# Half-height stacks: each head with 64 rows of its own in both stacks of a fused attention kernel

## The reference

```
scores = q @ k.T / sqrt(8)        # per head, 256 x 256 (short phases: 128 x 128)
attn = softmax(scores)
out = (attn @ v) @ Wo + bo + x    # then a norm
```

## Time and profile before

| | us |
|---|---|
| runs of the kernel (3) | 393.17, 393.67 (median), 396.62 |
| span of the profiled execution | 394.8 |
| TensorE matmul busy | 324.5 |
| VectorE busy | 291.2 |
| ScalarE busy | 233.6 |
| GpSimd busy | 182.8 |
| first maxima step | 35.15 |

### The profile page before, as it was taken

How to read it: one execution, slowest core, us unless ns; L and a number is a source line. 1 busy time by engine, 2 the same in 40 slices (tenths; PEclk the granted TensorE clock), 3 DMA queues, 4 the chain that set the end, 5 groups by cost and what they waited for, 6 DMA issues and landing times.

```text
span 394.8 us, 8256 instructions
## 1 busy us (share of the span) xinstructions
PE 324.5 (82%) x2838; PEld 195.7 (50%) x2838; DVE 291.2 (74%) x622; ACT 233.6 (59%) x502; POOL 182.8 (46%) x259
## 2 busy tenths in 40 slices
PE   0453678999998878969788898799999998999994
PEld 0230144555555546647556776474545544455551
DVE  4783967797995886967796538866888989898711
ACT  0220022767787753837378497468767775786692
POOL 8605015074341657857736255702667657550000
PEclk9995565999999998957899899899999999999998
DMA  7879309051746839189549143603447262544001
GB/s 246 316 94 123 24 9 114 2 95 32 120 67 60 105 47 93 27 109 114 97 61 113 16 84 83 79 2 83 88 51 107 47 77 63 62 87 53 15 3 28
DMA packets 39978, 30.54 MB, mean 77 GB/s; under 512 B 4352, under 2 KB 39040, under 8 KB 39808
## 3 DMA queue, kind: packets, MB, share of 16 engines
q1 hardware_dynamic: 39216, 28.66, 47.8%
q10 hardware_dynamic: 720, 1.35, 1.0%
HBM read 5.55 MB, written 0.52 MB: 15 GB/s over the span
## 4 chain that ended last, share of the span: by engine, by line
PE 47%; DVE 23%; DMA 10%; issue 9%; SPq 5%; ACT 4%; POOL 2%; ACTq 0%; POOLq 0%; DVEq 0%
PE ps_small L854 14%; PE ps_max L854 11%; DVE neg_max L1212 10%; PE ps_score L854 9%; PE ps_heads L854 9%; DMA q_stack<-q_parts 6%; SPq L724 3%; DVE k_parts L644 2%; DMA q_stack<-max_rows 2%; SPq L727 2%; DVE k_parts L642 2%; DVE onehot L1159 2%; PE ps_small L1001 2%; ACT probs L1052 1%; DMA pos_i<-in_pos 1%
## 5 line engine op out<-in xcount | busy, mean ns | idle before, releaser
L1212 DVE TENSOR_REDUCE neg_max<-ps_max 128x2 f32<-128x512 f32 (+1 forms) x256 | 165.1, 686 | 40.6 <-PE ps_max L854 38.3
L1052 ACT ACTIVATE probs<-ps_score 128x512 f32<-128x512 f32 x256 | 136.3, 605 | 43.1 <-PE ps_score L854 42.5
L854 PE MATMUL ps_max<-k_stack,q_stack 96*128 96x512 bf16 (+1 forms) x320 | 99.5, 368 | 22.4 <-DVE neg_max L1212 11.2
L854 PE MATMUL ps_score<-q_stack,k_stack 100*128 100x256 bf16 (+1 forms) x640 | 84.5, 259 | 3.6 <-DMA q_stack<-max_rows 2.6
L854 PE MATMUL ps_heads<-probs,v_cols 128*32 128x256 f32 (+1 forms) x1280 | 70.5, 344 | 0.7 <-ACT probs L1052 0.7
L854 PEld LDWEIGHTS ps_score<-q_stack,k_stack 100*128 100x128 bf16 x640 | 52.7, 101 | 30.4 <-ACT probs L1052 9.7
L641 POOL TENSOR_TENSOR split_r<-q_f,k_parts 64x256 f32<-64x256 f32 x26 | 18.7, 720 | 100.3 <-issue 87.5
L854 PEld LDWEIGHTS ps_max<-k_stack,q_stack 96*128 96x128 bf16 x320 | 28.7, 102 | 64.1 <-DVE neg_max L1212 42.1
L854 PEld LDWEIGHTS ps_heads<-probs,v_cols 128*32 128x32 f32 x1280 | 33.1, 110 | 24.1 <-issue 10.5
L854 PE MATMUL ps_small<-src_t,w 128*128 128x256 f32 x96 | 30.3, 437 | 2.1 <-ACT src_t L1118 1.1
L826 POOL TENSOR_TENSOR rstd<-var_eps,minus_half 128x2 f32<-128x2 f32 x20 | 14.2, 712 | 38.3 <-DVE var_eps L1170 38.1
(11 more groups left out here) (119 smaller groups left out, 446.9 us busy)
## 6 DMA issues: line engine op xcount, KB each, us to landing
k_stack<-k_parts SPq DMA_DIRECT2D x120, 128.0 KB, 4.1
q_stack<-q_parts SPq DMA_DIRECT2D x120, 64.0 KB, 3.8
w<-in_w SPq DMA_DIRECT2D x1, 1024.0 KB, 9.5
rows<-in_rows ACTq DMA_DIRECT2D x1, 704.0 KB, 9.1
w<-in_w SPq DMA_DIRECT2D x1, 576.0 KB, 11.3
pos_i<-in_pos ACTq DMA_DIRECT2D x2, 256.0 KB, 6.2
ctx_t<-in_ctx_t SPq DMA_DIRECT2D x2, 256.0 KB, 8.0
src_t<-in_x_t SPq DMA_DIRECT2D x2, 256.0 KB, 9.1
```

What stands on the lines that cost most here:

```text
L854: return nc.tensor.matmul(out, lhs_t, rhs, start=start, stop=stop, **k)
L1052: nc.scalar.activation(probs[:, n % PROB_BUFS, :], ps_score[n % SCORE_BUFS][:, :], ACT.Exp, scale=SCALE).then_inc(exped, 1)
L1212: nc.vector.tensor_reduce(dst, src, AX.X, ALU.max, negate=True).then_inc(max_taken, 1)
```

## The change

Both stacks get 128 used rows: the 64 rows 64*parity + 8*d + slot belong to one head of the pair, with six slots of parts and two spare ones. Each head so has rows of its own, and a matmul reads one half of the partitions: rows 0 to 63 or 64 to 127, with the array as a tile of 64 rows by 128 columns at row 0 or 64.

- `k_parts` loses its second plane and its zeros, `k_stack` is half as wide: [128, 3, 8 pairs, 256]. A stack DMA writes rows slot, slot+8, ... (16 of them, 4 KB each) for q and for k.
- A max bank is one parity: in long phases one head with both query tiles (two matmuls of 256 columns), in short ones two heads of one parity with both tiles (four of 128). Bank i has parity i mod 2. A score bank is as big as before, in short phases two heads of one parity; bank c has parity c mod 2. The contraction is over 62 rows for the maxima and 64 for the scores.
- The maxima go into rows 62, 63, 126 and 127, by two DMAs. The ones and zeros of the spare rows of both stacks are loaded by four DMAs from an input, ahead of three of the four weight loads; the memsets are gone, and the first max step waits for the loads.
- k's first part is one ACT instruction, its split one step. VectorE does it for unit 0 and phases 1 and 2 (before: unit 0, and half of it in phases 1, 2 and 4).
- The planner's costs: 120 in place of 216 and 218 for max and score steps, 1300 in place of 650 for placing maxima, 720 in place of 1080 for k's ACT work, 1150 in place of 1100 for a split on VectorE, other start times. `WEIGHTS` is the same.

```diff
-SLOT_ROWS = 2 * DH
-MAX_ROW = SLOT_ROWS * len(SLOTS)
-MAX_ROWS = 4
+ROW_SLOTS = 8
+SPARE_SLOTS = (6, 7)
+HALF = P // 2
+MAX_ROW = HALF - 2
...
-SPLIT_ON_DVE = (("k", 1, 0), ("k", 2, 0), ("k", 4, 1))
+SPLIT_ON_DVE = (("k", 1), ("k", 2))
...
-        pe = {"max": 216, "score": 218, "value": 590 if short else 1020, "q": 440, "k": 440, "v": 430,
+        pe = {"max": 120, "score": 120, "value": 590 if short else 1020, "q": 440, "k": 440, "v": 430,
...
-    plan.free.update(dve=11500, pool=14500)
+    plan.free.update(dve=9500, pool=1000)
...
-        k_parts = sb("k_parts", [P, 2, PARTS, 2, T], BF16)
+        k_parts = sb("k_parts", [P, 2, PARTS, T], BF16)
         q_stack = sb("q_stack", [P, STACK_BUFS, PAIRS, T], BF16)
-        k_stack = sb("k_stack", [P, STACK_BUFS, H, T], BF16)
+        k_stack = sb("k_stack", [P, STACK_BUFS, PAIRS, T], BF16)
...
+        def half_rows(par, n=HALF):
+
+            return slice(HALF * par, HALF * par + n)
...
+            for kind, stack in ((0, q_stack), (1, k_stack)):
+                for slot in SPARE_SLOTS:
+                    sp.dma_start(stack[slot::ROW_SLOTS, :, :, :].rearrange("r b h t -> r b (h t)"),
+                                 a["spare"][kind, slot - SPARE_SLOTS[0]].bitcast(BF16).unsqueeze(1).broadcast_to(
+                                     [P // ROW_SLOTS, STACK_BUFS, PAIRS * T])).then_inc(spare_loaded, 16)
...
+                        if (part > 0) == rest:
+                            sp.dma_start(stack_of(kind, u)[slot::ROW_SLOTS, :, :], parts_of(kind, u)[part]
+                                         ).then_inc((q_placed if kind == "q" else k_placed)[buf], 16)
...
+                    for par in range(2):
+                        sp.dma_start(q_stack[HALF * par + MAX_ROW:HALF * (par + 1), u % STACK_BUFS, :, :],
+                                     max_rows[2 * PAIRS * par:2 * PAIRS * (par + 1), u % 2, :]
+                                     ).then_inc(max_placed[u % STACK_BUFS], 16)
...
+                    first_pair, par = divmod(i, 2)
+                    at = half_rows(par, MAX_ROW)
...
-                        last = mm(out[:, :], q_stack[0:MAX_ROW, buf, pair, qt * P:(qt + 1) * P],
-                                  k_stack[0:MAX_ROW, buf, 2 * pair:2 * pair + 2, :].rearrange("p a b -> p (a b)"))
+                        for qt in range(NT):
+                            last = mm(out[:, qt * T:(qt + 1) * T], stack_of("q", u)[at, first_pair, qt * P:(qt + 1) * P],
+                                      stack_of("k", u)[at, first_pair, :])
...
+                    first_pair, par = divmod(c, 2)
+                    at = half_rows(par)
...
                         for kt in range(NT):
-                            last = mm(out[:, kt * T:(kt + 1) * T], k_stack[0:SCORE_ROWS, buf, c, kt * P:(kt + 1) * P],
-                                      q_stack[0:SCORE_ROWS, buf, c // 2, :])
+                            last = mm(out[:, kt * T:(kt + 1) * T],
+                                      stack_of("k", u)[at, first_pair, kt * P:(kt + 1) * P],
+                                      stack_of("q", u)[at, first_pair, :])
...
-                            for half, part in part_views(kind, u):
-                                last = nc.scalar.activation(part[0], ps_small[half, 0:T], ACT.Identity,
-                                                            bias=V(f"b{kind}{phase}")[half, :])
-                            last.then_inc(small_used[n % SMALL_BUFS], 1)
+                            nc.scalar.activation(parts_of(kind, u)[0], ps_small[:, 0:T], ACT.Identity,
+                                                 bias=V(f"b{kind}{phase}")).then_inc(small_used[n % SMALL_BUFS], 1)
```

More of the change, by code:

```diff
@@ L158, in waits @@
                 return [("part", kind[-1], u)]
-            return [("split" + kind[5:], u, half) for half in range(2 if kind == "stack_k" else 1)]
+            return [("split" + kind[5:], u)]
         if st[0] == "small" and self.count["small"] >= SMALL_BUFS:
@@ L294, in append @@
         if kind == "stack_max":
-            done["placed", "max", u] = run("dma", t, 650) + 2000
+            done["placed", "max", u] = run("dma", t, 1300) + 2000
             return
@@ L333, in append @@
             else:
-                t = part = run("act", t, 720 if kind == "q" else 1080)
+                t = part = run("act", t, 720)
             done["part", kind, u] = part
@@ L556, in build @@
         q_split = [sem(f"q_split{i}") for i in range(2)]
-        k_split = [[sem(f"k_split{half}{i}") for i in range(2)] for half in range(2)]
+        k_split = [sem(f"k_split{i}") for i in range(2)]
         base_ready = sem("base_ready")
@@ L622, in first_part_done, with split_done, split @@
             return used(no("small", kind, u)) if u // B else (first_part, 2 * u + turn(kind, u))
[L624 to L632, removed]
+        def split_done(kind, u):
+            return (q_split if kind == "q" else k_split)[u % 2], u // 2 + 1
+        def split(engine, ops, link, kind, u):
             which = 0 if kind == "q" else 1
@@ L638, in split @@
                 engine.wait_ge(s_, 16 * len(SLOTS) * n_)
-            lines, part = part_views(kind, u)[half]
-            full, rest = q_f[lines, u % 2, which, :], split_r[lines, u % 2, which, :]
+            part = parts_of(kind, u)
+            full, rest = q_f[:, u % 2, which, :], split_r[:, u % 2, which, :]
             link(ops.tensor_tensor(rest, full, part[0], ALU.subtract))
             link(ops.tensor_tensor(part[1], full, part[0], ALU.subtract))
-            done = split_done(kind, u, half)
+            done = split_done(kind, u)
             ops.tensor_tensor(part[2], rest, part[1], ALU.subtract).then_inc(done[0], 1)
@@ L1379, in constants @@
 def constants():
+    spare = np.zeros((2, len(SPARE_SLOTS), 2, DH, PAIRS * T), np.float32)
+    spare[1, :, :, DH - 1, :] = 1.0
+    spare = (spare.reshape(2, len(SPARE_SLOTS), P // ROW_SLOTS, PAIRS * T).view(np.uint32) >> 16).astype(np.uint16)
     iota = np.arange(MAX_POS, dtype=np.float32).reshape(POS_CHUNKS, P).T
```

116 lines of the change are left out of this document (41 added, 75 removed).

## The result

| | before | changed | ratio |
|---|---|---|---|
| first measurement, median (us) | 394.26 | 405.21 (400.86 to 416.07) | 1.019 [1.012, 1.026] |
| second measurement, median (us) | 393.85 | 403.95 (401.13 to 407.63) | 1.024 [1.017, 1.031] |

The changed kernel is slower by about 2%, some 10 us, where 381 us was forecast. It lies outside the range of 368 to 400.

The account below looks back on a forecast made before the run. TensorE's steps were taken to set the pace in the two full stretches. Terms -7 -2.8 -3 -1.5 +1 = -13.3 us from the 394.8 span gave 381.5, about 381 us for the median; range 368 to 400.

Parts of the forecast that it names:

- The order: TensorE's step order under the planner's new costs: scores shift 0 to 16 steps, ten steps some 3 us either way.
- Rival C: VectorE, the new order or colder TensorE stretches take back 8 to 12 us: 391 us, no change; chance 0.18.
- Parts 1 and 2: TensorE's maxima and scores: array shape changes +19.1 us, overlap of opposite halves -27.4; -8.3 together, taken at 85% as -7.
- Parts 3 to 6: Start -2.8 us, splits and first parts -3, later stack DMAs -1.5, maxima in two DMAs +1; together -6.3.
- part 3: The start: smaller key stacks land in 3.8 us, issues begin 0.42 earlier, first maxima at 32.3; -2.8 us, bounds 0 and -5.
- Part 5: Stack DMAs after the start: smaller transfers land sooner, cutting TensorE's waits for stacks; -1.5 us, bounds 0 and -3.4.
- Part 6: Placing the maxima by two DMAs: a second issue of 0.67 us on the SP queue, 20 times; +1 us, bound 13.4.
- The memsets on GpSimd held up nothing: At the start, GpSimd's first split waited 11.8 us for ACT's part of k, so dropping memsets gains nothing.
- Rival A: TensorE's changes of shape are paid and the overlap does not come: 404 us, slower; chance 0.13.
- Rival B: Half and full height are one shape for TensorE's drain, so no change cost: 364 us; chance 0.09.
- The signs that were named: Trace checks: first maxima near 32.3 us, overlapped starts, projections 0.10 late, less VectorE, GpSimd and ACT work, TensorE below 95%.

## Why the prediction was wrong

- **The order.** "At the clock's full level ten steps are some 3 us, either way; this I put in the range." This is the step that failed. The order was priced as steps shifted in a row of work, but it decides what stands beside each wait. It costs 20 us at full height (393.7 against 373.9) and 23 at half height (404 against 380.9). Rival C named the new order, with 8 to 12 us for three causes together; it had the right mechanism at less than half its size, and came out at 391, no change.
- **Parts 1 and 2**, -7 forecast, +7 to +10 measured: a second step that failed. The steps' prices were right: 0.10 per change, 0.107 for a matmul beside another. Missing were 0.10 more in the first projection behind half-height steps (some 85 places, 8 us if none were hidden), VectorE, whose wait (4.5 us for 0.2) took back most of the 5.6 us that TensorE was busy less in the last stretch, and the granted clock. The forecast held the clock fixed; with half heights it is lower in both orders (0.956 to 0.925, 0.937 to 0.884).
- **Parts 3 to 6**, -6.3 forecast, about -20 measured (373.9 for before's 394). The sign was right and the size was a third. The first maxima came 6.05 us earlier (29.10 for 35.15), not 2.8. The landing of the twelfth stack DMA went from 6.14 to 2.80 us, where part 3 had 3.8, and the issues began 2.64 earlier (19.12 for 21.76), where it had 0.42. The rule of the Trainium skill (SBUF — State Buffer, "Door 1: the DMA port swizzle") was the better guide for the landing: the kernel with every sixth row shows it fall from 4.1 to 2.4 in the median at the same bytes. The ports themselves no run shows. It was only with the earlier issues that the start passed the forecast's bound of -5. Part 5 (-1.5) counted TensorE's waits for stacks alone; the spread rows are worth 12 us, and only 3.8 of them come at the start. Part 6 (+1) did not come: in the order of before TensorE waits 0.8 us for placed maxima, with two DMAs, where it was 2.6.
- **"The memsets on GpSimd held up nothing"** was wrong. VectorE's one-hot instructions beside them ran slower (below), TensorE's first matmul on the one-hot matrix moved from 14.3 to 10.0 us, and k's first part, ahead of the stacks, from 20.89 to 18.68. The kernel with spread rows keeps the memsets, and its issues begin at 21.75 as before. How much of the 2.64 they are, no run shows alone.
- **Rival A** gave 404, the measured number, by luck: its mechanism is refuted, since the overlap came. **Rival B** is refuted by the 0.31 between the scores and the projection.
- **The signs that were named.** Overlapped starts and the 0.10 at projections held; GpSimd's -48 and ACT's -7.5 came near the 30 to 45 and 9 forecast. TensorE was busy below 95% in 65 to 145, as said (73.3 of 80), but it was so before (74.3 of 80), and the sign tells nothing. VectorE lost 19 us and not 10: its splits of k took 14.7 us for 27.4, and its work at the start some 5 less. The test for C, VectorE over 90% busy, looked for the wrong sign: its wait was in bursts of maxima at an average of 72.6 of 100.

What stays open: why the clock is lower with half heights. The same order at full height, half height with overlap and half height without it shows 0.937, 0.884 and 0.75 to 0.81, so it goes with the shape and not with the list of steps alone. The first and the last of these compute other numbers than the changed kernel (the exponent's scale is tiny), but since one has the highest clock and the other the lowest, the numbers do not explain it. Whether the fewer rows at work or the drains between shapes bring it down was not tried. Nor was the order repaired for half heights, with a table fitted to them; the lowest times here of kernels that leave nothing out are 380.9 (the changed kernel in the order of before) and 382.1 (the kernel before with spread rows), 3% under before.

## What to carry to other kernels

Where a planner with a fitted table makes the order, every edit of its costs, or of the steps it sees, is a new order: write out the old list and measure the edit in it before judging it, and then the order by itself. Place the rows of an SBUF-to-SBUF transfer far apart where the layout leaves a choice; here every sixth row in place of neighbours gave 12 us and needed no new instruction. And before shortening TensorE's steps, look at what it would wait for next and at its granted clock: time taken off there came back here as waits for VectorE and as work at 1.2 GHz.

## What the runs showed of the hardware

Two bf16 matmuls on rows 0 to 63 and 64 to 127 start within 0.02 us of each other, also from different steps into different banks (71.42 and 71.44 above). GpSimd's memsets slow some of VectorE's work beside them. VectorE's four one-hot instructions in the kernel before, with GpSimd setting the stacks beside them and later, with GpSimd idle; then in the changed kernel, which has no such memsets:

```profile
9.53 4.65 DVE L1159 TENSOR_SCALAR onehot<-pos_f,const 128x512 bf16<-128x512 f32 x4
...
48.26 1.67 DVE L1159 TENSOR_SCALAR onehot<-pos_f,const 128x512 bf16<-128x512 f32 x4
```

```profile
8.20 1.67 DVE L1129 TENSOR_SCALAR onehot<-pos_f,const 128x512 bf16<-128x512 f32 x4
```

The cast ahead of them went from 1.05 to 0.43, but an addition of two tensors between the two took 0.69 in both kernels. And a busy TensorE is not a warm one: between 117 and 127 us it was busy 9.74 of 10 us at a granted clock of 0.50, behind five microseconds in which it was busy 3.74 and the clock had begun to fall (0.82).
